# A two-layer graph network on one core: four scattered groups moved from the last half tile of the edge pass to the 23rd tile of the second layer

## The reference

```python
h = relu(layernorm(x))
# layer 0: out[s] += dinv[s] * w * dinv[d] * (h @ kernel)[d]  over edges (and self loops)
x = x + relu(out + bias)
h = relu(layernorm(x))
# layer 1: messages both ways, [h[heads], E] @ W_fwd + b_fwd to the tails,
#          [h[tails], E] @ W_back + b_back to the heads, then the mean at each node
agg = segment_sum(messages, msg_dst) / (cnt + AGG_EPS)
y = where(agg >= 0, agg, 0.01 * agg) + h
x = x + gamma * (y - mean(y)) * rsqrt(var(y) + LN_EPS) + beta
```

## Time and profile before

| | us |
|---|---|
| median of 3 runs | 4291.05 (4282.30 to 4295.39) |
| the profiled execution | 4283.32 |
| its span, from first to last instruction | 4281.5 |

### The profile page before, as it was taken

One profiled execution on the slowest core, in us unless ns is written; L12 is line 12 of the kernel. 1 busy time (PEld: TensorE's weight loads), 2 busy tenths in 40 slices (PEclk: granted clock), 3 DMA queues, 4 the chain that ended last, 5 costly groups with the idle time before them and its releaser, 6 DMA issues. The chain is left out here.

```text
span 4281.5 us, 100129 instructions
## 1 busy us (share of the span) xinstructions
PE 3343.3 (78%) x30312; PEld 2791.7 (65%) x30528; DVE 3161.2 (74%) x8053; ACT 1868.7 (44%) x4498; POOL 2999.1 (70%) x1809
## 2 busy tenths in 40 slices
PE   1454699888889888889923598889888888899964
PEld 1344577777777777777813477667767776777653
DVE  6999888888888888888825776666666666677527
ACT  1031355555555555555515244444444444445523
POOL 2666588888888888888840788777777777788301
PEclk9989899999999999999966699999999999999987
DMA  9992688777788778777876455445445544555761
GB/s 174 266 236 15 136 143 143 142 133 143 135 140 142 140 135 144 138 138 142 143 153 171 81 85 84 76 77 79 81 74 78 78 80 75 79 81 85 109 133 31
DMA packets 711723, 505.09 MB, mean 118 GB/s; under 512 B 305599, under 2 KB 617342, under 8 KB 711048
## 3 DMA queue, kind: packets, MB, share of 16 engines
q0 software_dynamic: 257584, 176.81, 37.2%
q1 hardware_dynamic: 453592, 321.45, 29.3%
HBM read 284.31 MB, written 240.17 MB: 122 GB/s over the span
## 5 line engine op out<-in xcount | busy, mean ns | idle before, releaser
L1632 POOL DMA_INDIRECT gcn_sums<-shared,ds_to_i x752 | 1289.6, 1715 | 515.5 <-ACT shared L1883 297.9
L806 POOL DMA_INDIRECT gcn_sums<-fl_sums,fl_to_i x864 | 1441.3, 1668 | 287.5 <-DMA gcn_sums<-fl_sums,fl_to_i 155.8
L1838 PE MATMUL bank<-ds_counts,ds_parts 128*128 128x256 bf16 x3675 | 605.2, 278 | 0.0
L1907 ACT COPY ds_turned<-bank 128x1024 bf16<-128x1024 bf16 (+1 forms) x325 | 313.1, 963 | 615.5 <-PE bank L1823 615.5
L1034 ACT COPY fl_sums<-bank 128x256 f32<-128x256 f32 x864 | 324.7, 376 | 567.3 <-PE bank L962 503.6
L1871 ACT CAST ds_counts<-bank 128x392 bf16<-128x392 f32 x800 | 382.2, 490 | 225.7 <-PE bank L1782 213.0
L844 DVE SCALAR_TENSOR_TENSOR fl_same<-fl_key_b,fl_pat,bank 128x128 f32<-128x128 bf16 x864 | 370.4, 441 | 104.4 <-PE bank L962 85.7
L1858 PE MATMUL bank<-ds_turned,ds_now 128*128 128x512 bf16 (+1 forms) x1734 | 427.7, 377 | 11.4 <-issue 0.2
L1767 DVE TENSOR_TENSOR src_sums<-src_sums,bank 128x512 f32<-128x512 f32 (+1 forms) x325 | 213.1, 656 | 281.1 <-PE bank L1858 276.4
L1800 PE MATMUL bank<-shared 128*128 128x128 f32 x1504 | 307.7, 309 | 119.7 <-DVE attr_sums L1684 91.7
L1697 DVE SCALAR_TENSOR_TENSOR shared<-shared,ds_pat,from_me 128x128 f32<-128x128 bf16 x752 | 312.7, 442 | 108.1 <-PE bank L1802 96.4
(11 more groups left out here) (254 smaller groups left out, 6927.2 us busy)
## 6 DMA issues: line engine op xcount, KB each, us to landing
fl_attrs<-in_edge_attr SPq DMA_DIRECT2D x108, 512.0 KB, 4.8
shared<-in_edge_attr SPq DMA_DIRECT2D x186, 256.0 KB
fl_rel_b<-dst_offset SPq DMA_DIRECT2D x108, 256.0 KB
fl_key_b<-src_key SPq DMA_DIRECT2D x108, 256.0 KB
gcn_sums<-zeros SPq DMA_DIRECT2D x40, 640.0 KB
shared<-src_key SPq DMA_DIRECT2D x94, 256.0 KB, 3.9
gcn_sums<-fl_sums,fl_to_i POOLq DMA_INDIRECT x864
near<-src_float SPq DMA_DIRECT2D x1, 12892.0 KB
```

Of the source, the lines that this page charges most:

```text
L806: nc.gpsimd.indirect_dma_start(out=d.tab_gcn[j % K], out_offset=bass.IndirectOffsetOnAxis(ap=to_i[:, (GPI * kk + gi) % 4, j:j + 1], axis=0 ...
L1632: nc.gpsimd.indirect_dma_start(out=d.tab_gcn[j % K].rearrange("n (two f) -> (n two) f", two=2), out_offset=bass.IndirectOffsetOnAxis(ap=to ...
L1838: ins = nc.tensor.matmul(row_bank[:, 0:2 * P], parts[:, tile, s, :], counts[:, h, tile, :, :].rearrange("p b q -> p (b q)"), start=(tile = ...
```

## The change

`G1` goes from 108 to 104 groups: the last slot of the first layer has none. `NB` goes from 94 to 98 and `BT` from 22 to 23: tile 22 of the second layer gets four groups beside it, among them the last, partly filled group. In the first layer slot 26 keeps its 13 turns, copies, products and adds. In the second layer the loops now cover the pairs 1 to 10 (tiles 2 to 21), and tiles 22, 23 and 24 are written out; `load_table` stands behind the groups of tile 22.

```diff
-G1 = GPI * (2 * DS + 1)
+G1 = GPI * 2 * DS
...
+        def ends_groups(i, kk):
+
+            return isinstance(i, int) and 2 * i + kk == 2 * DS - 1
...
-                for gi in range(GPI):
+                for gi in range(0 if last else GPI):
...
-                    if j == 0:
+                    if j == 0 and not last:
                         spot_sums(group(i, kk, gi), gi % 2)
-                    if j == 0 and not (first and gi == 0):
+                    if j == 0 and not (first and gi == 0) and not (last and gi > 0):
                         add_window(group(i, kk, gi) - 1)
-                    if not (last and gi == GPI - 1):
+                    if not last and not (ends_groups(i, kk) and gi == GPI - 1):
                         prepare(i, kk, gi + 1, j, True)
...
-                    sum_chunk(i, kk, gi, j)
-                    if j == 1:
+                    if not last:
+                        sum_chunk(i, kk, gi, j)
+                    if j == 1 and not last:
                         spread(i, kk, gi, 1)
...
-            with eng.Fori(1, BT // 2 - 1) as i:
+            with eng.Fori(1, BT // 2) as i:
                 pair_of_tiles(i, 0, True, False)
                 pair_of_tiles(i, 1, True, False)
-            pair_of_tiles(BT // 2 - 1, 0, True, False)
-            pair_of_tiles(BT // 2 - 1, 1, True, False)
+            pair_of_tiles(BT // 2, 0, True, False)
             if between:
                 between()
...
-            pair_of_tiles(SUPER // 2 - 1, 0, False, False)
-            pair_of_tiles(SUPER // 2 - 1, 1, False, False)
+            pair_of_tiles(BT // 2, 1, False, False)
             pair_of_tiles(SUPER // 2, 0, False, True)
...
+            for gi in range(GL):
+                scatter_group(BT // 2, 0, gi)
```

More of the change, by code:

```diff
@@ L931, in _ @@
             loop(dve, slot)
-            add_window(G1 - 1)
         @block.tensor
@@ L1002, in slot @@
                     gi, j = divmod(c, J)
-                    sum_chunk(i, kk, gi, j)
-                    if j == 1:
+                    if not last:
+                        sum_chunk(i, kk, gi, j)
+                    if j == 1 and not last:
                         spread(i, kk, gi, 1)
-                    if j == U + 1 and not (last and gi == GPI - 1):
+                    if j == U + 1 and not last and not (ends_groups(i, kk) and gi == GPI - 1):
                         spread(i, kk, gi + 1, 0)
@@ L1056, in slot @@
                     gi, j = divmod(c, J)
-                    keep_sums(i, kk, gi, j, first)
-                    if j == 1:
+                    if not last:
+                        keep_sums(i, kk, gi, j, first)
+                    if j == 1 and not last:
                         make_pay(i, kk, gi, 1)
-                    if j == U + 1 and not (last and gi == GPI - 1):
+                    if j == U + 1 and not last and not (ends_groups(i, kk) and gi == GPI - 1):
                         make_pay(i, kk, gi + 1, 0)
```

## The result

The changed kernel takes 4266.66 us (median of 7 runs, 4258.38 to 4271.69), the kernel before 4291.05 on the same chip (7 runs, 4280.46 to 4296.04): ratio 0.9942 (95% interval 0.9928 to 0.9955). It is faster by 24.4 us, where 11.7 were forecast, and lies 0.3 us outside the range given. The profiled execution took 4264.14 us, its span is 4262.3; the spans differ by 19.2 us, because the profiled execution of before lay 7.7 us under its median and this one 2.5. On the third chip of the experiments, three timed runs (two of the changed kernel, one with four tiles a pass) took 4311 to 4330 us; they are left out of the medians given here.

The account below looks back on a forecast made before the run. POOL's scatters were taken to end the first layer, PE and its partners to set the second layer's tile length. -59.5 + 7.3 + 20 + 20.5 = -11.7 us moves the median from 4291.05 to 4279.4, range 4267 to 4293.

Parts of the forecast that it names:

- Part 1: Last slot of the first layer: without its 32 scatters on POOL it ends earlier, -59.5 us (ends -60.5 and -57).
- the near tie of products and traffic: End of the first layer: last products done at 2139.1 us, scatter traffic at 2138.0, equal within what could be told.
- They take 142.15 instead of 134.81: Second layer: tiles 20 and 21, now in the loop, take the length of a loop pair, +7.3 us.
- Part 2: Second-layer loop: one more jump back, as tiles 20 and 21 move into it, +7.3 us (ends 5 and 8).
- Part 3: Tile 22 of the second layer: with groups it takes 67.4 instead of 47.35 us, +20 (ends 18.5 and 21.5).
- Part 4: End of the second layer: table loads, hidden by 26 us before, now end last, +20.5 us (ends 17 and 22).
- The DMA share of 0.99: Accumulating table loads: they already fill the DMA engines at 0.99, so should be no faster than 27 us apart.
- the chain did not stay hidden: Rival at the table loads: landing in under 20 us each, they add nothing; -32 us, about 4259; chance 0.04.
- The products ran slow: Rival in the first layer's last slot: without groups PE's clock drops and products run slow, over 2.2 us apart; chance 0.07.
- POOL didn't fall behind: Rival in tile 22: POOL's full scatter backlog adds 20 us, sum +8, about 4299; decides from 22 us lag; chance 0.07.
- The last slot did get shorter by the time of its scatters: Rival in the first layer: something other than POOL ends slot 26, so no gain; 0.06 including anything unseen.
- the four terms: Whole kernel: last slot -59.5, jump back +7.3, tile 22 +20, table chain +20.5, together -11.7 us.

Follow-up runs that it names:

- the shorter loop: Changed kernel with tiles 20 and 21 of the second layer written out again, one jump back fewer; 4244.1 us, ratio 0.99 to the kernel before.
- slot 64: Kernel before with only the head of PE's second-layer loop set at program slot 64, same instructions; 4283.73 us, ratio 0.9991.
- slot 160: Kernel before with only the head of PE's second-layer loop set at program slot 160, same instructions; 4265.74 us, ratio 0.9958.

## Why the prediction was right and wrong

- **Part 1** (-59.5): right, -59.7 and -60.9. Both the 60 us less of scatters and the near tie of products and traffic stood as worked out (add over at 2150.2, traffic at 2151.7).
- **The step that failed**: the sum had terms only for the stages that the diff touches, and put tiles 4 to 19 at nothing without a reason. They carried -17.7 us (-13.0 on the first chip), more than the whole forecast gain. "They take 142.15 instead of 134.81" shows how: the length of a pair in the loop was taken for a property of the work, and it was one of that build's placement. In the changed kernel a pair takes 139.94, in the loop's 16 old tiles as in the new two: PE's loop stands at another place, and PE stops once behind a jump and not twice. Part of the evidence was at hand: the rows of "issue" (2.26 us) and of a granted clock of 0.76 behind a jump back said that the loop's cost isn't in its instructions, and the change takes code away ahead of that loop. The tile that I had looked at, 16, is one of the two mildest of the eight (72.26 us, the mean is 73.8), and its second stop of 1.0 us, and the second stops at all the other jumps, escaped me.
- **Part 2** (+7.3): near, +5.2 and +7.3, and the shorter loop gives back 7.1. The direction and the jump are right. The size is partly luck: 4.4 us are in the tile behind the jump, the rest in tile 21, whose written-out length differs by 1.8 us from profile to profile.
- **Part 3** (+20): right, +20.3 and +20.2.
- **Part 4** (+20.5): right, +20.0 and +19.7, with the loads 26.8 us apart. But one reason given for it was a misreading. The DMA share of 0.99 is a mean over the 27 us of one load, and a share adds up the times of packets, so that it can pass 1 (1.43 in the second window here). Windows of the kernel before (columns as in rows 1) take it apart:

```profile
4044.00:4049.00 5.00, 4.61 (x48) 3.22 (x48) 3.37 (x4) 3.23 (x8) 4.38 (x1) 1.00 0.00 0
4050.00:4065.00 15.00, 14.21 (x148) 10.34 (x149) 8.26 (x11) 9.09 (x17) 0.00 (x0) 1.00 1.43 176
```

  In the first 5 us of this load nothing moves, while POOL issues it (4.38 us), and then it moves 176 GB/s. At 5 us each the chain of three loads stands still for some 15 us (an estimate), and the trace doesn't show that the engines could take no more: the plain load of table 0 moves the same 3200 KB in 14.4 us in the changed kernel. An accumulating one takes 26.2 us to landing there and 26.8 from one to the next.
- **The rivals**: the chain did not stay hidden (tail 27.5). The products ran slow for one step of 2.8 us and not for twelve: PE paused for 1.45 us, the granted clock was 0.57 from 2124 to 2128 us, and from 2128 to 2148 us it was 1.00. POOL didn't fall behind (9.4 us; it would have decided from 22). The last slot did get shorter by the time of its scatters.
- **The rest**: measured, the four terms give -59.7 + 5.2 + 20.3 + 20.0 = -14.2 us. With -17.7 for tiles 4 to 19, +13.1 of setup, -0.5 of tile 23 and +0.1 elsewhere it is -19.2, the difference of the spans. The medians differ by 24.4 us in that session, 39.6 on the first chip and 26.0 on the third. Of the 14 to 15 us between these gains the longer setup makes about 12; the rest wasn't traced further.

The forecast of the direction of each part held. The gain forecast was too small because the change moved a loop as well as groups; that it wasn't further off is luck, since setup happened to give 13 us of it back.

## What to carry to other kernels

A change in an early section can alter the time of an untouched loop behind it by moving that loop in the program: compare stage by stage, the untouched ones too, and give the sum a term for them when PE's trace shows idle time with "issue" at a loop's head, and look at every pass, not at one. Look for instruction packets among the DMA queues there. When a sum works, read which loop costs hide in it: here the loop's better place could be had alone (21 us). Three quarters of the first layer's gain were lost to the jump, tile 22 and the table chain; the chain's part came back with plain loads and adds in place of accumulating ones. A mean over a window can hide that part of it is empty: cut a share of 0.99 into pieces before it is called full.

## What the runs showed of the hardware

- A jump back of PE's loop was followed by 1.9 to 4.3 us of idle time with "issue" as its only reason, and a granted clock of 0.57 to 0.86 over 12 us (tile 10 of four profiles), made up of stretches at 0.50 and at 1.00; the same instructions take 1119.7 or 1140.2 us over 16 tiles by the place of the loop's head.
- Each of these stops ends 1.3 to 2.4 us after a packet of 16384 bytes on the queue "instruction" 8 (first stops of before and the changed kernel 1.6 to 1.7). In the kernel before there are two such stops behind a jump (3.0 to 4.3 us together), with the head at slot 64 one of 2.7 to 3.9 us behind two packets, with slot 160 and in the changed kernel one of 1.9 to 2.7.
- In the changed kernel a load of 3200 KB that accumulates into SBUF follows the last one after 26.8 us: some 5 us in which next to nothing moves (5 GB/s from 4026 to 4031 us), then 176 GB/s (4032 to 4047). A plain load of the same bytes lands after 14.4 us. Three tables in 12 plain pieces, with POOL's adds of 3.7 us in the mean beside them, take 61.8 us from the first issue (4005.5) to the last add (4067.3), 20.6 us a table.
- The DMA share of a window can exceed 1 (1.43 here) and can be 0.99 over a window whose first 5 us are empty.
- PE stopped for up to 5.8 us (four tiles a pass; 5.2 in the changed kernel) with "issue" as the reason and no packet of queue 8, while the transfers moved 393 and 394 GB/s (shares of 1.02 and 1.01). The changed kernel stopped so in two sessions (setup 488.2 and 487.7 us) and not in a third (476.3).
